# Projections with their loads ahead of the key arrays, and attention sums with the attention term broadcast as rows

## The chip, the cores and the metric

The kernel runs on one core of a Trainium2 chip. The metric is device time of one execution in microseconds (us): the median of three timed runs. One further execution was taken by the hardware profiler; all rows of the trace come from it.

## The reference

Two graph layers over 12500 nodes of 256 numbers and 200000 edges, sorted by `dst`:

```python
# layer 0: attention of each node `dst` over its edges
enh = x + 0.1 * query_emb
Q, K, V = enh @ Wq + bq, enh @ Wk + bk, enh @ Wv + bv           # (N, 4 heads, 64)
scores = sum_d Q[dst] * (K[src] + 0.2 * rel_w[edge_type]) / 8   # one per edge and head
w = softmax of scores over the edges of one dst
msgs = segment_sum(w * V[src], dst)                             # V where a node has no edge
y = layernorm(msgs @ Wo + bo + x) * gamma + beta
x = layernorm(x + y)
# layer 1: sums over the edges of one src
x_i, x_j = leaky(x @ W1 + b1), leaky(x @ W2 + b2)
a1, a2 = x_i @ wa1 + ba1, x_j @ wa2 + ba2
att = sigmoid(a1[src] + a2[dst])                                # one per edge
x = layernorm(2 * x + segment_sum(att * x_j[dst], src))
```

## The kernel before

Nodes lie in 98 blocks of 128; a table in SBUF, `node_tab`, holds 260 columns for each block. Edges are sorted by the node that they are summed into and cut into tiles of 128. Merged with the block borders they give 1664 steps: one tile against one block, four steps (U) to a group, 416 groups (G). The stages follow one another, each a block of the program with a barrier behind it:

1. `project` (L200 to L392): Q into `node_tab`, K and V to DRAM as `kv_rows`. At the same time VectorE starts to sort 200000 keys (node pair, for the second layer), 1024 columns to an operation.
2. `build_steps` for layer 0: which block each step works on (`places`), the local number of each edge's node (`local`), the other end of each edge (`other`).
3. `edge_scores`: GpSimd gathers K and V of each step by indirect DMA (L645), TensorE picks Q rows with a one-hot, VectorE multiplies and reduces and, between groups, goes on with the key sort (L717, L719).
4. `softmax_numerators`, then `aggregate`: V rows weighed by ScalarE and GpSimd, summed by TensorE with a one-hot (L1027) and added to `node_tab` by VectorE (L1006).
5. `build_steps` for layer 1, `update_nodes`: Wo, two layer norms, W1 and W2, a1 in `a1_tab` (one column to a block), rows x_j with a2 as column 256 to DRAM as `xj_rows`.
6. `attend`: the sums of layer 1, then `finish`: the last layer norm.

In `project`, SyncE first issues the loads of the key arrays (after GpSimd has padded them), `keys[n][0:97]` at L243 and the rest at L244, then weights and biases (L247, L248), the query column (L250) and the blocks of x (L254), two in flight. GpSimd splits the biases into three bf16 parts. For each block TensorE turns x (L339), ScalarE adds 0.1 query on the way from PSUM (L310), TensorE multiplies by Wk, Wv (L352, 512 columns) and Wq (L352, 256 columns) and adds the bias by a matmul of ones with the three parts (L353, one for K and V, one for q). ScalarE evacuates q scaled by 1/8 (L317) and K, V (L319), GpSimd stores them (L295). There is one PSUM tile for turned x and one for q, two for K, V.

In `attend`, the groups pass through the engines with these hand-overs. GpSimd gathers four times 128 rows of `xj_rows` (L1340) into a ring of RING = 6 groups; before group g it waits for the sum of group g - 6. VectorE makes the one-hot of the local number against `iota` (L1371, two groups ahead), TensorE turns it (L1407), ScalarE copies the turned one (L1360), TensorE multiplies it with the block's column of `a1_tab` (L1427): a1 of each edge. VectorE adds a2 (L1377), ScalarE takes the sigmoid (L1348) and scales the one-hot with it (L1353), TensorE sums 128 rows of x_j with it (L1415, each fp32 product is two matmul records), VectorE adds the result to `node_tab` (L1386), whose place is loaded to registers from `places1`. TensorE's order is turn(g + 1), lookup(g), sum(g - 1); VectorE's is one-hot(g + 2), a2 of g, add(g - 2).

## Time and profile before

| | us |
|---|---|
| median of 3 timed runs | 7487.49 |
| lowest, highest | 7469.43, 7493.04 |
| the profiled execution | 7541.05 |
| its span, first to last instruction | 7539.4 |
| busy: TensorE 71%, VectorE 60%, GpSimd 55%, ScalarE 41% of the span | 5366.9, 4547.7, 4117.2, 3080.2 |

Engines in the rows: PE is TensorE (PEld its weight loads), DVE VectorE, ACT ScalarE, POOL GpSimd, SP SyncE; SPq is SyncE's own queue, which issues DMAs. L352 is line 352 of the kernel before. Busy time is that of the engine, so an issue of an indirect DMA on POOL counts, one on SPq does not. Times of the trace are counted from the first instruction.

### The profile page before, as it was taken

The page shows a single profiled execution, that of the slowest core. Times are in us where ns is not written, and L with a number is a line of the kernel's source. Part 1 is how long each engine was busy: PE and PEld are TensorE (multiplying, and loading weights), DVE is VectorE, ACT ScalarE, POOL GpSimd, SP SyncE. Part 2 cuts the span into 40 slices and gives each one's busy share as a digit, 9 for nine tenths or more (in the row PEclk, how much of TensorE's full clock was granted, in tenths as well). Part 3 has the DMA queues.
Part 4 walks back from the last instruction along what each step waited for, and adds up shares of the span by engine and source line. Part 5 has one row for each costly group of instructions (what it writes and reads, how often), then busy time and mean ns, then how long its engine had stood idle before and what let it go on. Part 6 is the DMA issues. An engine that isn't in the chain of part 4 may idle for free. (4 is left out here: it accounts for less than half of the span.)

```text
span 7539.4 us, 82733 instructions
## 1 busy us (share of the span) xinstructions
PE 5366.9 (71%) x21563; PEld 4019.8 (53%) x21563; DVE 4547.7 (60%) x8352; ACT 3080.2 (41%) x8260; POOL 4117.2 (55%) x4183
## 2 busy tenths in 40 slices
PE   5966666666667556637777768877777777777874
PEld 2445555555555444425555544446666666666663
DVE  6216666767677555578888878964444444444446
ACT  2323333333333333328777754433333333333333
POOL 1126666666667555513333325556666666666663
PEclk9976776767666676669999999987777777777776
DMA  2348888888898888816666643323333333333333
GB/s 74 106 146 281 276 292 285 276 287 289 291 299 290 287 280 275 274 36 199 199 199 199 199 142 88 88 78 92 91 91 91 91 91 91 91 91 91 91 92 112
DMA packets 857534, 1308.71 MB, mean 174 GB/s; under 512 B 87145, under 2 KB 690535, under 8 KB 856787
## 3 DMA queue, kind: packets, MB, share of 16 engines
q0 software_dynamic: 221008, 683.55, 29.1%
q1 hardware_dynamic: 629091, 613.77, 26.1%
q10 hardware_dynamic: 7010, 6.38, 0.2%
q8 instruction: 187, 3.06, 0.2%
q14 instruction: 238, 1.95, 0.1%
HBM read 1031.10 MB, written 272.26 MB: 173 GB/s over the span
## 5 line engine op out<-in xcount | busy, mean ns | idle before, releaser
L645 POOL DMA_INDIRECT s_rows<-kv_rows,other x1664 | 1737.3, 1044 | 949.3 <-issue 496.1
L1340 POOL DMA_INDIRECT t_rows<-xj_rows,other x1664 | 1626.0, 977 | 837.5 <-issue 444.6
L1415 PE MATMUL ps_xsum<-t_rows,t_hot_att 128*128 128x256 f32 x3328 | 1235.7, 536 | 417.5 <-DVE node_tab L1386 388.7
L754 PE MATMUL ps_rel<-rel,hot 64*128 64x64 f32 x3328 | 613.0, 341 | 862.6 <-DVE s_rows L737 628.5
L756 PE MATMUL ps_q<-node_tab,hot 128*128 x3328 | 1191.6, 518 | 36.1 <-issue 35.6
L1415 PEld LDWEIGHTS ps_xsum<-t_rows,t_hot_att 128*128 128x128 f32 x3328 | 863.8, 272 | 594.6 <-issue 356.1
L754 PEld LDWEIGHTS ps_rel<-rel,hot 64*128 64x128 f32 x3328 | 552.3, 249 | 1057.2 <-issue 969.3
L734 DVE TENSOR_TENSOR s_rows<-s_rows,ps_rel 128x1024 f32<-128x1024 f32 x416 | 506.4, 1217 | 931.8 <-remote 706.7
L661 ACT ACTIVATE hot<-apart,ones 128x1024 f32<-128x1024 bf16 x416 | 477.8, 1148 | 1373.3 <-remote 767.7
L1027 PE MATMUL ps_sum<-a_terms,a_hot 128*128 128x260 f32 x3328 | 830.1, 392 | 282.7 <-DVE node_tab L1006 193.3
L756 PEld LDWEIGHTS ps_q<-node_tab,hot 128*128 128x128 f32 x3328 | 817.3, 258 | 221.0 <-issue 42.6
L987 ACT ACTIVATE a_terms<-a_terms,score 128x64 f32<-128x64 f32 x3328 | 839.8, 334 | 218.8 <-DMA a_terms<-v_edges 218.1
L1386 DVE TENSOR_TENSOR node_tab<-node_tab,ps_xsum 128x256 f32 x1664 | 699.9, 421 | 363.1 <-issue 181.1
L1027 PEld LDWEIGHTS ps_sum<-a_terms,a_hot 128*128 128x128 f32 x3328 | 599.3, 190 | 513.3 <-issue 430.2
L1006 DVE TENSOR_TENSOR node_tab<-node_tab,ps_sum 128x260 f32 x1664 | 703.5, 423 | 183.0 <-DVE node_tab L1006 5.4
L972 POOL TENSOR_TENSOR a_terms<-a_terms,score 128x512 f32<-128x512 f32 x416 | 438.2, 1053 | 661.6 <-DMA a_terms<-v_edges 661.6
L1377 DVE TENSOR_TENSOR t_logit<-ps_a,t_rows 128x4 f32<-128x4 f32 x416 | 67.4, 162 | 1084.0 <-DMA x_in<-in_x 1036.4
L1360 ACT COPY t_node_hot<-ps_hot 128x512 f32<-128x512 f32 x416 | 243.8, 586 | 915.9 <-remote 831.9
L656 ACT ACTIVATE apart<-apart,minus_p 128x1024 bf16<-128x1024 bf16 x416 | 473.4, 1138 | 326.6 <-DMA apart<-what_rows 239.4
L1353 ACT ACTIVATE t_hot_att<-t_hot,t_att 128x128 f32<-128x128 f32 x1664 | 531.6, 390 | 13.6
L737 DVE TENSOR_TENSOR s_rows<-s_rows,ps_q 128x1024 f32<-128x1024 f32 x416 | 507.8, 1221 | 14.2
L739 DVE TENSOR_REDUCE score<-s_rows 128x16 f32<-128x1024 f32 x416 | 507.4, 1220 | 14.2
(208 smaller groups left out, 5835.0 us busy)
## 6 DMA issues: line engine op xcount, KB each, us to landing
v_edges<-s_rows SPq DMA_DIRECT2D x416, 512.0 KB
a_terms<-v_edges SPq DMA_DIRECT2D x416, 512.0 KB, 3.7
apart<-what_rows SPq DMA_DIRECT2D x416, 256.0 KB
s_rows<-kv_rows,other POOLq DMA_INDIRECT x1664
t_rows<-xj_rows,other POOLq DMA_INDIRECT x1664
kv_rows<-kv_out POOLq DMA_DIRECT2D x97, 256.0 KB, 2.3
xj_rows<-n_hx SPq DMA_DIRECT2D x97, 130.0 KB, 2.1
x_in<-in_x SPq DMA_DIRECT2D x97, 128.0 KB, 2.0
```

The costliest lines, as they stand in the source:

```text
L645: pool.indirect_dma_start(out=rows[g % KV_RING][:, k, :], out_offset=None, in_=t["kv_rows"], in_offset=bass.IndirectOffsetOnAxis(ap=t["oth ...
L737: dve.tensor_tensor(key, key, ps_q[g % 2][:, :, :], ALU.mult).then_inc(picked_used, 1)
L739: dve.tensor_reduce(t["score"][:, g * U * H:(g + 1) * U * H].rearrange("p (k h) -> p k h", h=H), by_head, AX.X, ALU.add)\
L754: nc.tensor.matmul(ps_rel[g % 2][:, k, :], hot[g % 2][0:R, 1, k, :], rel_02[:, :], start=True, stop=True)
L756: last = nc.tensor.matmul(ps_q[g % 2][:, k, :], hot[g % 2][:, 0, k, :], t["node_tab"][:, bass.ds(blocks[k] * AW, D)], start=True, stop=True)
L987: last = nc.scalar.activation(head, head, ACT.Copy, scale=t["score"][:, at:at + 1])
L1006: dve.tensor_tensor(acc, acc, ps_sum[g % 2][:, k, 0:AW], ALU.add).then_inc(added, 1)
L1027: last = nc.tensor.matmul(ps_sum[g % 2][:, k, 0:AW], hot[g % 4][:, k, :], terms[g % DEEP][:, k, :], start=True, stop=True)
L1340: pool.indirect_dma_start(out=rows[g % RING][:, k, :], out_offset=None, in_=t["xj_rows"], in_offset=bass.IndirectOffsetOnAxis(ap=t["other1 ...
L1353: last = nc.scalar.activation(hot_att[g % 2][:, k, :], hot[g % 4][:, k, :], ACT.Copy, scale=att[g % 2][:, k:k + 1])
L1386: dve.tensor_tensor(acc, acc, ps_sum[g % 2][:, k, :], ALU.add).then_inc(added, 1)
L1415: last = nc.tensor.matmul(ps_sum[g % 2][:, k, :], hot_att[g % 2][:, k, :], rows[g % RING][:, k, 0:D], start=True, stop=True)
```

## The change

In `project`: SyncE issues block 0 of x, the query column and the weights first, then three more blocks of x, the three biases broadcast to 128 partitions, and then the keys, each array as 96 rows, one row and the rest; it also issues the stores of K and V, from four buffers instead of two. x has four buffers, all three kinds of PSUM tile have two. The bias matmuls and the bf16 parts are gone: VectorE evacuates K and V with a tensor_tensor that adds the bias, and q with a scalar_tensor_tensor that scales and adds. The key sort is a generator, of which VectorE runs one operation after each K/V evacuation and, in two blocks of three, one more after q, from block 6 on.

In `build_steps` for layer 1, one operation makes `block_hot`: for each step a column with a 1 at its block. In `attend`, a1 is turned to rows (98 x 128), multiplied by `block_hot` to one row of 128 for each step, and stored to DRAM as `a1_rows`. For each group SyncE broadcasts four of these rows to all partitions, eight groups in flight. ScalarE takes sigmoid(a1 row + a2 of the gathered edge) over 128x128; VectorE multiplies it with the one-hot in one scalar_tensor_tensor, in place; TensorE sums. All hand-overs are by step, VectorE's adds lag three groups and alternate with the weighing, PSUM has four tiles, the ring of gathered rows RING = 14 groups. The lookup of a1 by TensorE, its copy and the logits are gone. Tiles of layer 0 are given back sooner, and `update_nodes` has a scratch tile of its own.

```diff
-RING = 6
+RING = 14
+ATT_RING = 8
@@ project, SyncE
+            load(0)
+                sp.dma_start(q_col[:, :], query.rearrange("(c p) -> p c", p=P)).then_inc(weights_in, 16)
+            for n, w in ((1, wk), (2, wv), (0, wq)):
+                sp.dma_start(w_qkv[:, :, n * D:(n + 1) * D], w.rearrange("(c p) n -> p c n", p=P)).then_inc(weights_in, 16)
+            for b in range(1, 4):
+                load(b)
+            for n, a in enumerate((bq, bk, bv)):
+                sp.dma_start(b_wide[:, n * D:(n + 1) * D], a.partition_broadcast(P)).then_inc(biases_in, 16)
             sp.wait_ge(pads_set, 1)
             for n, a in enumerate((t["src"], t["dst"])):
-                sp.dma_start(keys[n][0:full_p, :], a[0:full_p * F].rearrange("(p f) -> p f", f=F)).then_inc(keys_in, 16)
+                sp.dma_start(keys[n][0:even_p, :], a[0:even_p * F].rearrange("(p f) -> p f", f=F)).then_inc(keys_in, 16)
+                sp.dma_start(keys[n][even_p:full_p, :], a[even_p * F:full_p * F].rearrange("(p f) -> p f", f=F)).then_inc(keys_in, 16)
...
+            for b in range(NB):
+                if b + 4 < NB:
+                    sp.wait_ge(xt_ready, b + 1)
+                    load(b + 4)
+                r = rows_of(b)
+                sp.wait_ge(kv_ready, b + 1)
+                sp.dma_start(t["kv_rows"][b * P:b * P + r, :], kv_out[b % 4][0:r, :]).then_inc(kv_stored[b % 4], 16)
@@ project, TensorE
-                        nc.tensor.matmul(o, enh[u][:, c, :], w_qkv[:, c, lo:hi], start=(c == 0), stop=False)
-                    last = nc.tensor.matmul(o, t["ones_h"][0:3, :], b_parts[:, lo:hi], start=False, stop=True)
+                    last = nc.tensor.matmul(ps_kv[b % 2][:, :], enh[b % 2][:, c, :], w_qkv[:, c, D:3 * D], start=(c == 0), stop=(c == 1))
...
+                    last = nc.tensor.matmul(ps_q[b % 2][:, :], enh[b % 2][:, c, :], w_qkv[:, c, 0:D], start=(c == 0), stop=(c == 1))
@@ project, VectorE
+            for b in range(NB):
+                dve.wait_ge(kv_done, b + 1)
+                if b >= 4:
+                    dve.wait_ge(kv_stored[b % 4], 16 * (b // 4))
+                dve.tensor_tensor(kv_out[b % 4][:, :], ps_kv[b % 2][:, :], b_wide[:, D:3 * D], ALU.add).then_inc(kv_ready, 1)
+                if b >= 6:
+                    next(sorting, None)
+                dve.wait_ge(q_done, b + 1)
+                dve.scalar_tensor_tensor(tab[:, b * AW:b * AW + D], ps_q[b % 2][:, :], float(DH) ** -0.5, b_wide[:, 0:D],
+                                         ALU.mult, ALU.add).then_inc(q_kept, 1)
+                if b >= 6 and b % 3:
+                    next(sorting, None)
+            for _ in sorting:
+                pass
@@ build_steps
+            if layer:
+                step(dve.tensor_scalar(t["block_hot"][:, :], row, partition[:, 0:1], None, ALU.is_equal))
@@ attend, SyncE
+            for n, (lo, hi) in enumerate(halves):
+                sp.wait_ge(a1_copied, n + 1)
+                sp.dma_start(t["a1_rows"][lo * P:hi * P, :].rearrange("(c p) e -> p c e", p=P), a1_steps[:, lo:hi, :]).then_inc(a1_stored, 16)
+            sp.wait_ge(a1_stored, 2 * 16)
+            for g in range(G):
+                if g >= ATT_RING:
+                    sp.wait_ge(summed, (g - ATT_RING + 1) * U)
+                sp.dma_start(att[g % ATT_RING][:, :, :].rearrange("p k e -> p (k e)"),
+                             t["a1_rows"][g * U:(g + 1) * U, :].rearrange("k e -> (k e)").partition_broadcast(P)).then_inc(a1_in[g % ATT_RING], 16)
@@ attend, GpSimd
-                    pool.wait_ge(summed, g - RING + 1)
+                    pool.wait_ge(summed, (g - RING + 1) * U)
@@ attend, ScalarE
+                act.wait_ge(a1_in[g % ATT_RING], 16 * (g // ATT_RING + 1))
+                act.wait_ge(rows_in[g % RING], 16 * U * (g // RING + 1))
                 for k in range(U):
+                    last = nc.scalar.activation(att[g % ATT_RING][:, k, :], att[g % ATT_RING][:, k, :], ACT.Sigmoid,
+                                                bias=rows[g % RING][:, k, D:D + 1])
+                last.then_inc(att_ready, 1)
@@ attend, VectorE
+            def weigh(g, k):
+                if k == 0:
+                    dve.wait_ge(att_ready, g + 1)
+                w = att[g % ATT_RING][:, k, :]
+                dve.scalar_tensor_tensor(w, t["iota"][:, :], t["local1"][:, g * U + k:g * U + k + 1], w, ALU.is_equal, ALU.mult)\
+                    .then_inc(hot_att_ready, 1)
+
+            def add(g, k, block):
+                acc = tab[:, bass.ds(block * AW, D)]
+                dve.wait_ge(summed, g * U + k - k % 2 + 2)
+                if g * U + k:
+                    dve.wait_ge(added, g * U + k)
+                dve.tensor_tensor(acc, acc, ps_sum[g % 4][:, k, :], ALU.add).then_inc(added, 1)
+
+            for g in range(G + 3):
+                if g >= 3:
+                    blocks = blocks_of(nc, dve, t["places1"], g - 3)
                 for k in range(U):
+                    if g < G:
+                        weigh(g, k)
+                    if g >= 3:
+                        add(g - 3, k, blocks[k])
@@ attend, TensorE
+            nc.tensor.transpose(ps_a1, t["a1_tab"][:, :], t["ident"][:, :]).then_inc(a1_turned, 1)
+            pe.wait_ge(a1_staged, 1)
+            for n, (lo, hi) in enumerate(halves):
+                for c in range(lo, hi):
+                    last = nc.tensor.matmul(ps_steps[n][:, c - lo, :], t["block_hot"][0:NB, c * P:(c + 1) * P], a1_stage[:, :], start=True, stop=True)
+                last.then_inc(a1_spread, 1)
+            pe.wait_ge(a1_copied, 2)
+            for g in range(G):
                 for k in range(U):
+                    pe.wait_ge(hot_att_ready, g * U + k + 1)
+                    if g >= 4:
+                        pe.wait_ge(added, (g - 4) * U + k - k % 2 + 2)
+                    nc.tensor.matmul(ps_sum[g % 4][:, k, :], att[g % ATT_RING][:, k, :], rows[g % RING][:, k, 0:D], start=True, stop=True)\
+                        .then_inc(summed, 1)
```

## Rows read from the trace of the kernel before

**Rows 1.** Busy time by stretch: stretch, us, engines' busy us, clock, DMA share, GB/s.
```profile
77.00:445.00 368.00, 363.50 (x1176) 168.72 (x1176) 161.72 (x142) 136.32 (x392) 53.07 (x98) 1.00 0.30 104
...
3367.00:4480.00 1113.00, 830.11 (x3328) 599.34 (x3328) 928.84 (x2080) 876.61 (x3743) 438.17 (x416) 1.00 0.63 197
...
4994.00:7459.00 2465.00, 1900.60 (x8320) 1593.41 (x8320) 1017.67 (x2496) 841.38 (x2497) 1625.95 (x1664) 0.74 0.34 91
```

**Rows 2.** Waits of the first 77 us: total us, times, longest.
```profile
ACT q L304 <- DMA q_col<-in_L_gnn_query_emb: 69.0, 1, 69.0
DVE keys L367 <- DMA keys<-in_dst: 68.5, 1, 68.5
```

**Rows 3.** Timeline of the start: start us, us, engine, line, work.
```profile
13.98 28.33 SPq L244 DMA_DIRECT2D keys<-in_dst  x1
...
60.33 2.41 SPq L250 DMA_DIRECT2D q_col<-in_L_gnn_query_emb  x1
...
79.14 3.62 PE L352 MATMUL ps_kv<-w_qkv,enh 128*128 128x512 f32 x4
```

**Rows 4.** Timeline of TensorE over one block of the projections.
```profile
92.70 1.88 PE L352 MATMUL ps_kv<-w_qkv,enh 128*128 128x512 f32 x4
...
94.51 0.39 PE L353 MATMUL ps_kv<-b_parts,ones_h 3*128 3x512 bf16 x1
...
94.83 1.13 PE L352 MATMUL ps_q<-w_qkv,enh 128*128 128x256 f32 x4
...
95.89 0.28 PE L353 MATMUL ps_q<-b_parts,ones_h 3*128 3x256 bf16 x1
...
96.10 0.44 PE L339 MATMUL ps_xt<-ident,x_in 128*128 128x128 f32 x2
...
96.38 1.88 PE L352 MATMUL ps_kv<-w_qkv,enh 128*128 128x512 f32 x4
```

**Rows 5.** Timeline of the next stage's start, three loads of 768 KB.
```profile
454.64 0.38 SPq L452 DMA_DIRECT2D score<-in_dst  x1
...
466.09 0.17 DVE L506 TENSOR_SCALAR last_block<-score 128x13 int32<-128x13 int32 x1 [224.78 <-DMA score<-in_edge_type]
```

**Rows 6.** Timeline of VectorE and GpSimd: attention sums, then edge scores.
```profile
6002.22 0.95 POOL L1340 DMA_INDIRECT t_rows<-xj_rows,other  x1 [0.31 <-issue]
6002.33 0.68 DVE L1371 TENSOR_TENSOR t_hot<-iota,local 128x512 f32<-128x512 f32 x1
...
6008.24 0.68 DVE L1371 TENSOR_TENSOR t_hot<-iota,local 128x512 f32<-128x512 f32 x1
...
6008.48 1.27 POOL L1340 DMA_INDIRECT t_rows<-xj_rows,other  x1 [0.30 <-issue]
...
1011.00 1.22 DVE L717 TENSOR_TENSOR keys<-keys 128x1024 f32<-128x1024 f32 x1
...
1011.07 1.96 POOL L645 DMA_INDIRECT s_rows<-kv_rows,other  x1 [0.30 <-issue]
```

**Rows 7.** Timeline of GpSimd in the attention sums, a gather that waited.
```profile
6035.14 0.95 POOL L1340 DMA_INDIRECT t_rows<-xj_rows,other  x1 [1.83 <-PE ps_xsum L1415]
```

**Rows 8.** Groups of instructions by line: shapes, count, busy us, mean ns, idle before.
```profile
L1386 DVE TENSOR_TENSOR node_tab<-node_tab,ps_xsum 128x256 f32 x1664 | 699.9, 421 | 363.1 <-issue 181.1 <-DVE node_tab L1386 3.4 <-remote 1.2
...
L1353 ACT ACTIVATE t_hot_att<-t_hot,t_att 128x128 f32<-128x128 f32 x1664 | 531.6, 390 | 13.6
...
L1231 DVE TENSOR_TENSOR n_hx<-ps_h,n_hx 128x512 f32<-128x512 f32 x98 | 66.4, 678 | 7.1 <-ACT n_hx L1145 7.0
...
L1298 DVE SCALAR_TENSOR_TENSOR score<-n_v,n_alone,score 128x256 f32<-128x256 f32 x98 | 43.9, 448 | 0.1
```

**Rows 9.** Two lines of the sums: ns min/median/max, first and last start us.
```profile
L1371 DVE TENSOR_TENSOR t_hot<-iota,local x416: 681/684/694, 4993.8 to 7443.8; 128x512 f32<-128x512 f32 x139
...
L1340 POOL DMA_INDIRECT t_rows<-xj_rows,other x1664: 940/947/1554, 4994.5 to 7439.0; - x185
```

**Rows 10.** Timeline, the last adds of the attention sums.
```profile
7456.67 2.11 DVE L1386 TENSOR_TENSOR node_tab<-node_tab,ps_xsum 128x256 f32 x4 [0.21 <-DVE node_tab L1386]
```

More of the change, by code:

```diff
@@ L204, in sb, with pb @@
             return ctx.enter_context(nc.sbuf_tensor(name, shape, dt))
+        def pb(name, shape):
+            return [ctx.enter_context(nc.psum_tensor(f"{name}{u}", shape, fp32)) for u in range(2)]
         def sem(name):
@@ L227, in project @@
[L227 to L233 removed]
+        b_wide = sb("b_wide", [P, 3 * D])
@@ L356, in _, with transpose @@
-            transpose(0, 0)
-            block_pairs(pe, body)
+            def transpose(b):
+                pe.wait_ge(x_loaded[b % 4], 16 * (b // 4 + 1))
+                if b >= 2:
+                    pe.wait_ge(enh_ready, b - 1)
+                for c in range(2):
+                    last = nc.tensor.transpose(ps_xt[b % 2][:, c, :], x_in[b % 4][:, c * P:(c + 1) * P], ident[:, :])
+                last.then_inc(xt_ready, 1)
+            pe.wait_ge(consts_set, 1)
+            transpose(0)
@@ L393, in _, with sort @@
-            assert now == MERGES[0][1]
+            def sort():
+                step = Serial(dve, key_step)
+                dve.wait_ge(keys_in, 6 * 16)
+                dve.wait_ge(consts_set, 2)
+                dve.tensor_scalar(keys[0][:, :], keys[0][:, :], NODE_BITS, KEY_BIAS, ALU.logical_shift_left, ALU.bitwise_or).then_inc(key_step, 1)
+                yield
+                dve.wait_ge(key_step, 1)
+                dve.tensor_tensor(keys[0][:, :], keys[0][:, :], keys[1][:, :], ALU.bitwise_or).then_inc(key_step, 1)
+                yield
+                step.n = 2
+                for m in range(7):
+                    step(dve.tensor_scalar(pbit[:, m:m + 1], pid[:, :], m, 1, ALU.logical_shift_right, ALU.bitwise_and))
+                step(dve.tensor_scalar(sign[:, 0:7], pbit[:, 0:7], -2.0, 1.0, ALU.mult, ALU.add))
+                step(dve.memset(sign[:, 7:8], 1.0))
+                step(dve.tensor_tensor(two_signs[:, 0:7], sign[:, 0:7], sign[:, 1:8], ALU.mult))
+                yield
+                done, now = step.n, 0
+                for k in range(1, FREE + 1):
+                    z = pair[now]
+                    if k == 1:
+                        v = z.rearrange("p (n s w) -> p n s w", s=2, w=2)[:, :, 1, :]
+                    elif k < FREE:
+                        v = z.rearrange("p (n s w) -> p n s w", s=4, w=1 << (k - 1))[:, :, 1:3, :]
+                    else:
+                        v = z[:, F // 2:F]
+                    dve.wait_ge(key_step, done)
+                    dve.tensor_scalar(v, v, -1.0, None, ALU.mult).then_inc(key_step, 1)
+                    done += 1
+                    yield
+                    if k == FREE:
+                        dve.wait_ge(key_step, done)
+                        dve.tensor_scalar(z, z, sign[:, 0:1], None, ALU.mult).then_inc(key_step, 1)
+                        done += 1
+                        yield
+                    for j in range(k - 1, -1, -1):
+                        a, b = (v.rearrange("p (n two d) -> p n two d", two=2, d=1 << j) for v in (pair[now], pair[1 - now]))
+                        dve.wait_ge(key_step, done)
+                        dve.tensor_tensor(b[:, :, 0, :], a[:, :, 0, :], a[:, :, 1, :], ALU.min)
+                        yield
+                        dve.tensor_tensor(b[:, :, 1, :], a[:, :, 0, :], a[:, :, 1, :], ALU.max).then_inc(key_step, 1)
+                        done += 1
+                        now = 1 - now
+                        yield
+                assert now == MERGES[0][1]
+                dve.wait_ge(key_step, done)
@@ new lines, in _ @@
+            sorting = sort()
+            dve.wait_ge(biases_in, 3 * 16)
+            dve.wait_ge(bias_ready, 1)
+            for b in range(NB):
+                dve.wait_ge(kv_done, b + 1)
[9 more added lines that the diff above has]
+                    next(sorting, None)
@@ L1328, in attend @@
[L1328 to L1332 removed]
+        att = [sb(f"t_att{u}", [P, U, P]) for u in range(ATT_RING)]
@@ new lines, in attend @@
+        a1_stage, a1_steps = sb("t_a1_stage", [NB, P]), sb("t_a1_steps", [P, C, P])
+        ps_sum = [ctx.enter_context(nc.psum_tensor(f"ps_xsum{u}", [P, U, D], fp32)) for u in range(4)]
+        ps_a1 = ps_sum[3][0:NB, 0, 0:P]
+        ps_steps = [ps_sum[u][:, :, :].rearrange("p k (two e) -> p (k two) e", e=P) for u in range(2)]
+        halves = ((0, 8), (8, C))
+        rows_in, a1_in = [sem(f"t_rows_in{u}") for u in range(RING)], [sem(f"t_a1_in{u}") for u in range(ATT_RING)]
+        a1_turned, a1_staged, a1_spread, a1_copied, a1_stored = (sem(f"t_a1_{n}") for n in ("turned", "staged", "spread", "copied", "stored"))
@@ L1388, in _ @@
-            encode(0)
-            encode(1)
-            for g in range(G):
-                if g + 2 < G:
-                    encode(g + 2)
-                add_logits(g)
-                if g >= LAG:
-                    add(g - LAG)
-            for g in range(G - LAG, G):
-                add(g)
+            def weigh(g, k):
[4 more added lines that the diff above has]
+                    .then_inc(hot_att_ready, 1)
```

253 lines of the change are left out of this document (60 added, 193 removed).

## The prediction, made before the changed kernel was run

> **What bounds the kernel now.** I read the stage table first. Cut by stage, the span shows two stretches that the change rewrites: the first stage, up to 445 us, and the attention sums from 4994 to 7459 us, 2465 us or 33% of the span [rows 1]. The other stages (edge scores, softmax, first aggregation, node update, finish) keep their code.
>
> The waits of the start come next: ScalarE sat 69.0 us for the query column, VectorE 68.5 us for the keys [rows 2]. The timeline says why: SyncE puts the two key arrays into its queue first, one issue alone takes 28.33 us, the query column goes out at 60.33 and the first K/V projection starts at 79.14 [rows 3]. After that TensorE is busy 363.5 of 368 us [rows 1]: the projections are bound by TensorE, one block of 128 nodes every 3.68 us (92.70 to 96.38) [rows 4]. VectorE is not the bound there: its key sort ended 224.78 us before 466.09, at 241.3 [rows 5].
>
> In the attention sums no engine is full: TensorE 1901, GpSimd 1626, VectorE 1018, ScalarE 841 of 2465 us [rows 1]. A group of four steps takes 2465/416 = 5.93 us. GpSimd issues gathers 1.25 us apart (0.95 and 0.30 between) as long as it need not wait [rows 6], and about once in eight gathers waits 1.8 us for a sum to free a ring place [rows 7]. So the pace comes from the loop TensorE (turn the one-hot, look up a1, sum) to ScalarE to VectorE and back. TensorE at its mean granted clock of 0.74 [rows 1] is close to full there: this loop, and not the gathers, ends last.
>
> **First stage: the loads.** In the new order block 0 of x, the query column and the three weights go out before anything else, and the keys last. Nothing waits for a 776 KB transfer any more. The query column takes 2.41 us to issue [rows 3]; a large load 0.38 us, and three of 768 KB landed 11.4 us after the first of their issues [rows 5], so 0.9 MB of x and weights need some 5 us. From a first issue near 1 us that gives 8 to 10, and I take 12 since each piece is small; the first K/V matmul then at 13 instead of 79.14 (1 us for the scaled column and the enhanced block 0). Bounds: 9 (the 8 us and the same 1) and 25 (x and weights share the queues with the keys). Gain 66 us, 54 to 70.
>
> **First stage: the blocks.** Both bias matmuls go: from 94.51 to 94.83 and from 95.89 to 96.10, 0.32 + 0.21 us of each period [rows 4]. 3.68 - 0.53 = 3.15; I take 3.2. VectorE takes over what ScalarE evacuated: the K/V add reads 512 columns of PSUM as L1231 does, 0.68 us, and q some 0.43 (L1298 has 0.45 for 256 columns, L1386 0.42) [rows 8]. With the sort (241.3 - 68.5 = 173 us over its 92 blocks, 1.88) that is 0.68 + 0.43 + 1.88 = 2.99 us a block, under 3.2 with PSUM two deep. The cover is thin, 0.2 us; if it is gone, VectorE sets 3.5 (0.68 + 0.43 + two sort operations of 1.2) and the stage gains 32 us less. 147 sort operations have 153 places, so none is left over. The keys must be there at block 6, at 13 + 6 x 3.2 = 32 us: in the next stage three loads of 768 KB, each split as the keys now are, were all there 11.4 us after the first issue (454.64 to 466.09) [rows 5], so two take some 8 us and land near 25. SyncE now also issues the stores of K/V; a store has two blocks of slack and GpSimd's issuing of them was hidden before. Blocks: 98 x 0.48 = 47 us. Together 66 + 47 = 113 us; from 54 + 18 = 72 to 70 + 52 = 122.
>
> A rule of the Trainium skill lies beside the 28.33 us: DMA: Bandwidth & Descriptors, on why a DMA increments its semaphore by 16, says that a copy is split over the largest number of engines up to 16 that divides its slowest dimension, thus 97 rows on one engine and 96 on sixteen. The keys' split into 96 + 1 rows would by it be quick; were it wrong, they would land near 70 us and hold VectorE, and through it TensorE, at block 6 for about 38 us, a third of the stage's gain. The three loads of [rows 5] are of the 128-row kind and bear the rule out.
>
> **Between.** `block_hot` is one tensor_scalar over 128x1664 on VectorE's path: 1 us, bounded by 0.3 and 2. The scratch tile, the other places of tiles and the longer list of semaphores to clear: 0 to 1 us each; 0.
>
> **Attention sums: what goes.** The encode (0.68 us), the 4 transposes and 8 lookup matmuls of a group, the copy and the logit go; TensorE keeps the 8 passes of the sum. In their place SyncE broadcasts 256 KB a group, ScalarE does four sigmoids of 128x128 (L1353 has 0.39 us each, 1.56 a group), VectorE four scalar_tensor_tensor of 128x128. L1298 takes 0.448 us for 256 columns; at 1.05 ns a column (1.22 us for 1024 columns, 0.684 for 512) [rows 6, 9] half of them is 0.31 us [rows 8].
>
> What sets the pace then? VectorE: 4 x (0.31 + 0.42) + 0.34 for the register loads + some 0.1 for each of 8 waits = 4.1 us, bounded by 3.3 (no gaps) and 5.3 (0.3 us of gap on every weigh, 0.15 on every add). TensorE: the first aggregation has the same 8 passes, the same adds and an encode besides, and took 1113/416 = 2.68 us a group at clock 1.00 [rows 1]; at half clock twice that share of it that is matmul, 830/416 x 2 = 4.0 us. ScalarE 1.6. DMA: 0.34 busy now at 91 GB/s [rows 1]; the rows add 256 KB per 5 us, 51 GB/s, so 0.6 at most. GpSimd: 4 x 1.252 = 5.01 us. All others lie below it, so GpSimd becomes the bound, and with 14 groups in the ring (70 us of gathers) it never waits for a sum: the 15 us that the a1 rows need to be spread, stored and read back (two copies of about 1 us, 26 passes, a store and a load of 3 to 4 us each) are hidden behind gathers that start at once. Without that cover they would cost their 15 us once.
>
> **Attention sums: the gather against VectorE.** A gather reads its indices from SBUF. Where an encode, which has two SBUF inputs, had started 0.24 us before a gather, the gather took 1.27 instead of 0.95 us; where the encode started 0.11 us after it, it took 0.95 [rows 6]. The same in the edge scores: an exchange of the key sort at 1011.00, the gather at 1011.07 took 1.96, until 0.8 us after the exchange had ended at 1012.22 [rows 6]. So a gather is held only if such an operation runs about 0.1 us after its start, and by what is left of it. The new weigh has two SBUF inputs as well, four of 0.31 us a group. At random phase 0.31/1.25 = 25% of gathers lose half of 0.31: 0.04 us each, 64 us in all. Bounds: nothing (the phase is locked, the weighs fall between the reads), and 0.31 on every gather, 516 us. I take 64, since the phase is locked to the landing of the rows and at most one or two of four read moments meet a weigh.
>
> SBUF — State Buffer of the Trainium skill, on its two separate sides, states more: the shared pair is an exclusive lock that whoever starts first holds for the whole instruction. Read so, a gather would also hold a weigh, up to 0.95 us. Here no encode was ever longer than 0.694 us, with one beginning 0.11 us into a gather [rows 6, 9]; the trace does not bear that half out for gathers. By the rule VectorE would need 0.36 us more a weigh (0.76 of the time inside a gather, 0.47 on average): 5.5 us a group, 200 us more than the sum below; that is part of the rival on VectorE's pace.
>
> **The sum.** First gather to last: 1663 x 1.252 + 64 = 2146 us instead of 7439.0 - 4994.5 = 2444.5 [rows 9], gain 298 (0 to 362 without the worst phase). Behind the last gather now come 20 us (the last adds end at 7458.8) [rows 10]; then landing 3, sigmoids 1.5, four weighs 3.5, the adds of three more groups 8.5: 17, gain 3. In all 113 + 298 + 3 - 1 = 413 us. The profiled execution took 7541 us (span 7539.4), so its successor takes 7128. The median of the three timed runs is 7487.5, 53.6 us below the profiled one; the same difference off it gives **7075 us**.
>
> **Rivals.** *VectorE or TensorE sets the pace of the sums* (semaphore round trips on each of 16 steps' hand-overs, or the half of the lock that I set aside): 5.3 to 5.6 us a group instead of 5.16, 60 to 190 us more; 7200. For it: three engines now pass each single step on; against it the 2.68 us of the first aggregation. *The first stage gains only its start*: VectorE, with the sort between the adds, holds TensorE at 3.5 to 3.7 us a block, or the keys come late: 7075 + 40 = 7115. *The other side*: each gather is met by a weigh. Phase is locked, so a bad phase would stay for all 416 groups. From 0.29 us a gather on (478 us over 1664) everything is lost; at 0.31 on each the sums take 2600 + 17 us, and the kernel 7075 + 452 = 7527, slower. Against it: a weigh of 0.31 us would have to begin just before every read, while weighs come some 0.9 us apart and gathers 1.25.
>
> **How the numbers follow.** Forecast 0.74 (own range 7010 to 7150), VectorE's or TensorE's pace 0.13, first stage short 0.09, the gathers all held 0.02, something else that costs over 400 us 0.02. What a measurement can tell from no change is 0.3%, 22 us. Faster 0.96, same 0.01, slower 0.03. The range for 8 in 10 is 7000 to 7210: its low end has no held gather and a stage at 3.1 us a block, its high end reaches into the paced rival.
>
> **What would show it.** Right: the first K/V matmul before 20 us and blocks 3.2 us apart; in the sums GpSimd busy about 0.76 of the stage, its gaps 0.30 us almost throughout, the group at 5.0 to 5.2 us, no wait for a sum; gathers with a second length up to 1.26 us. Wrong: gathers waiting for sums again; weighs longer than 0.35 us or starting late behind a gather; K/V adds that TensorE waits for; a stage of sums above 2300 us.

## The result, and the profile of the changed kernel

| | before | after |
|---|---|---|
| median, same chip | 7487.0 (4 runs) | 7281.5 (4 runs) |
| ratio, 95% interval | | 0.972 (0.971 to 0.974) |
| span of the profiled execution | 7539.4 | 7282.5 |
| first gather of the edge scores begins | 508.3 | 342.3 |
| first gather of the edge scores to the end of the last | 2686 | 2655 |
| first gather of the attention sums to the end of the last | 2445.5 | 2370.0 |

The gain is 205.5 us, where 413 were forecast. The profile of before lies 54 us above its median, so the traces differ by 257: 166 before the first gather of the edge scores, 31 in the edge scores, whose code is the same, 67 in the sums up to their last matmul, less 7 lost in the other stages.

The first stage did more than forecast. Its timeline in the changed kernel (start us, us, engine, line, work; the answer to [rows 3, 4]):

```profile
7.15 0.20 ACT L292 ACTIVATE q<-q_col 128x2 f32<-128x2 f32 x1 [5.13 <-DMA w_qkv<-in_L_gnn_Wq]
...
8.06 3.78 PE L325 MATMUL ps_node_kv<-w_qkv,enh 128*128 128x512 f32 x4
...
22.49 1.88 PE L325 MATMUL ps_node_kv<-w_qkv,enh 128*128 128x512 f32 x4
24.21 1.03 PE L330 MATMUL ps_node_q<-w_qkv,enh 128*128 128x256 f32 x4
25.07 0.38 PE L312 MATMUL ps_xt<-ident,x_in 128*128 128x128 f32 x2
25.29 1.02 PE L325 MATMUL ps_node_kv<-w_qkv,enh 128*128 128x512 f32 x2
```

The first K/V matmul starts at 8.06 instead of 79.14, and a block takes 2.80 us (22.49 to 25.29) instead of 3.68. By stretch, as in [rows 1] (stretch and its length, then busy us of TensorE, its weight loads, VectorE, ScalarE and GpSimd, each with its instructions; granted clock, DMA share, GB/s):

```profile
8.00:285.00 277.00, 276.36 (x977) 166.26 (x976) 255.38 (x351) 61.07 (x196) 0.00 (x0) 1.00 0.45 143
...
4810.00:7160.00 2350.00, 1195.02 (x3226) 729.47 (x3226) 1060.46 (x3214) 504.21 (x1632) 1580.48 (x1648) 0.66 0.49 140
```

TensorE is full in the first stage, VectorE nearly. In the sums nothing is: GpSimd 67%, TensorE 51%, VectorE 45%. A group takes 5.70 us, not the 5.16 of the forecast. The lines of the sums (the answer to [rows 8, 9]), and what GpSimd waited for between 4810 and 7160 (us in total, times, longest):

```profile
L1359 POOL DMA_INDIRECT t_rows<-xj_rows,other x1664 | 1595.9, 959 | 792.0 <-issue 470.7
...
L1392 DVE TENSOR_TENSOR node_tab<-node_tab,ps_xsum 128x256 f32 x1664 | 699.6, 420 | 1227.9 <-remote 848.4
...
L1384 DVE SCALAR_TENSOR_TENSOR t_att<-iota,local,t_att 128x128 f32<-128x128 f32 x1664 | 578.2, 348 | 77.8 <-issue 46.2
```

```profile
POOL t_rows L1359 <- issue: 466.4, 1526, 0.8
POOL t_rows L1359 <- remote: 248.1, 83, 9.2
POOL t_rows L1359 <- PE ps_xsum L1418: 51.7, 39, 4.1
```

No gather is held by VectorE (959 ns against 977), no weigh by a gather (348 ns). But GpSimd waits for sums again, with 14 places in its ring, and VectorE's adds wait 848 us for something that the profile calls "remote". The timeline shows such a wait:

```profile
5989.60 1.33 PE L1418 MATMUL ps_xsum<-t_rows,t_att 128*128 128x256 f32 x4 [1.04 <-issue]
5989.83 0.35 DVE L1384 SCALAR_TENSOR_TENSOR t_att<-iota,local,t_att 128x128 f32<-128x128 f32 x1
5990.21 0.96 POOL L1359 DMA_INDIRECT t_rows<-xj_rows,other  x1 [0.30 <-issue]
...
5995.27 0.95 POOL L1359 DMA_INDIRECT t_rows<-xj_rows,other  x1 [0.30 <-issue]
5996.48 0.32 SPq L1350 DMA_DIRECT2D t_att<-a_rows  x1
5996.53 0.96 POOL L1359 DMA_INDIRECT t_rows<-xj_rows,other  x1 [0.30 <-issue]
5996.59 0.42 DVE L1392 TENSOR_TENSOR node_tab<-node_tab,ps_xsum 128x256 f32 x1 [6.41 <-remote]
```

From 5990.9 to 5996.5 every engine but GpSimd stands still, and SyncE and VectorE go on together. VectorE was waiting for the sum of three groups back, whose matmul had ended at 5983.4, as had 11 later sums by 5991. So I compared the semaphore updates in the trace with the ends of the instructions that make them. An update is what an engine adds to a semaphore, its report to the others. In the stages without gathers an update comes 0.01 to 0.02 us after its instruction, on every engine. In the stages where GpSimd gathers, TensorE's come late, and TensorE's alone: in the changed sums 2.7 us behind the latest matmul at the median and 8.3 at the 95th percentile, VectorE's and ScalarE's 0.01 us (as far as their updates are recorded). The kernel before has it too, at the median 3.8 us behind the latest lookup, 2.6 behind the latest transpose, 1.5 behind the latest sum. There GpSimd paused after each eighth gather (205 times) and the updates came 1.5 us after that gather's end. What it waited for between 5010 and 7430:

```profile
POOL t_rows L1340 <- issue: 439.7, 1442, 0.4
POOL t_rows L1340 <- remote: 239.0, 129, 4.1
POOL t_rows L1340 <- PE ps_xsum L1415: 134.2, 75, 2.1
```

I had read these waits [rows 7] as a busy loop of engines.

### The profile page after: what moved, and what is told of

It reads as the page before. It is cut to its first block and busy times, and to the rows that moved or that the text cites. A ratio compares the mean times of both kernels' runs of the same rounds, so it can differ in the third digit from the quotient of the medians.

```text
span 7282.5 us, 70497 instructions
## 1 busy us (share of the span) xinstructions
PE 4567.1 (63%) x16402; PEld 3136.6 (43%) x16402; DVE 4715.6 (65%) x9381; ACT 2684.0 (37%) x7236; POOL 4037.0 (55%) x4077
## 5 line engine op out<-in xcount | busy, mean ns | idle before, releaser
L1359 POOL DMA_INDIRECT t_rows<-xj_rows,other x1664 | 1595.9, 959 | 792.0 <-issue 470.7
L1418 PE MATMUL ps_xsum<-t_rows,t_att 128*128 128x256 f32 x3328 | 1228.0, 516 | 1161.2 <-DVE t_att L1384 624.3
L1418 PEld LDWEIGHTS ps_xsum<-t_rows,t_att 128*128 128x128 f32 x3328 | 746.1, 248 | 1642.9 <-DVE t_att L1384 794.1
L1374 ACT ACTIVATE t_att<-t_att,t_rows 128x128 f32<-128x128 f32 x1664 | 514.0, 388 | 1856.7 <-DMA t_att<-a_rows 1615.4
L765 PE MATMUL ps_q<-node_tab,hot 128*128 x3328 | 1162.4, 507 | 39.6 <-issue 38.8
L763 PE MATMUL ps_rel<-rel,hot 64*128 64x64 f32 x3328 | 592.8, 333 | 861.8 <-DVE s_rows L746 648.4
L763 PEld LDWEIGHTS ps_rel<-rel,hot 64*128 64x128 f32 x3328 | 533.3, 241 | 1053.3 <-issue 947.1
L765 PEld LDWEIGHTS ps_q<-node_tab,hot 128*128 128x128 f32 x3328 | 797.7, 252 | 218.7 <-issue 48.3
L1384 DVE SCALAR_TENSOR_TENSOR t_att<-iota,local,t_att 128x128 f32<-128x128 f32 x1664 | 578.2, 348 | 77.8 <-issue 46.2
L1005 DVE TENSOR_TENSOR a_hot<-iota,keys 128x512 f32<-128x512 f32 x416 | 286.9, 690 | 0.0
```

Of the source, the lines that this page charges most:

```text
L763: nc.tensor.matmul(ps_rel[g % 2][:, k, :], hot[g % 2][0:R, 1, k, :], rel_02[:, :], start=True, stop=True)
L765: last = nc.tensor.matmul(ps_q[g % 2][:, k, :], hot[g % 2][:, 0, k, :], t["node_tab"][:, bass.ds(blocks[k] * AW, D)], start=True, stop=True)
L1359: pool.indirect_dma_start(out=rows[g % RING][:, k, :], out_offset=None, in_=t["xj_rows"], in_offset=bass.IndirectOffsetOnAxis(ap=t["other1 ...
L1374: last = nc.scalar.activation(att[g % ATT_RING][:, k, :], att[g % ATT_RING][:, k, :], ACT.Sigmoid, bias=rows[g % RING][:, k, D:D + 1])
L1384: dve.scalar_tensor_tensor(w, t["iota"][:, :], t["local1"][:, g * U + k:g * U + k + 1], w, ALU.is_equal, ALU.mult)\
L1418: nc.tensor.matmul(ps_sum[g % 4][:, k, :], att[g % ATT_RING][:, k, :], rows[g % RING][:, k, 0:D], start=True, stop=True)\
```

## The experiments

The sets ran on five chips, numbered 10, 3, 11, 14 and 4; each kernel is compared with the kernel before on its own chip. The changed kernel as it stands ran on chips 3 and 4; on 11 and 14 its figures are those of the first comparison, whose kernel before took nearly the same time (7487.0 beside 7492.4 and 7475.5). The expectations in us for set 1 were made for a chip where the kernel before takes 7487.

**Set 1, chip 10: each half alone, fewer reports, no gathers.** `e1` has the new first stage with the old sums, `e2` the reverse.

> The new first stage with the old attention sums (ring of 6). The traces of before and after put 195 us before the first gather of the attention sums. If that is so and independent of the sums: 7487 - 195 = 7292 us (7280 to 7310), blocks again 2.80 us apart. If by the forecast's sizes: 7374. If part of the gain came by way of the other edit, nearer 7400.

> The old first stage with the new attention sums. If the sums gave 75 us whatever stands before them: 7487 - 75 = 7412 us (7400 to 7430), the sums again some 2370 us from first to last gather. By the forecast (gathers set the pace): 7186.

`e3`:

```diff
-                    nc.tensor.matmul(ps_sum[g % 4][:, k, :], ...).then_inc(summed, 1)
+                    last = nc.tensor.matmul(ps_sum[g % 4][:, k, :], ...)
+                last.then_inc(summed, 1)
```

> The kernel after, but TensorE reports its sums once a group (on the last matmul) instead of once a step; VectorE, SyncE and GpSimd wait by group. Theory A (each TensorE semaphore update is held up while gathers are issued, and the updates queue up, so their number sets the pace): 416 updates instead of 1664, the sums fall toward the gathers' own 2100 us, the kernel to 7000 to 7100. Rival B (the hold-up is a delay of some us that does not depend on the number of updates): 7270 to 7300, as after. Rival C (TensorE's half clock after pauses is the cause): 7270 to 7320, or slower, since the adds of a group now start later.

`e4`:

```diff
-                    pool.indirect_dma_start(out=rows[g % RING][:, k, :], ..., in_=t["xj_rows"], ...)
+                    sp.dma_start(rows[g % RING][:, k, :], t["xj_rows"][lo:lo + P, :])
```

> The kernel after with the gathers of the attention sums left out: SyncE loads as many rows (128 rows of 1040 bytes a step, contiguous, other rows than the right ones), GpSimd stands still. It tells whether the gathers or something among the engines keeps TensorE's reports back. Theory A: TensorE's updates come within 0.1 us of its matmuls, a group takes 2.7 to 3.5 us, the kernel 6100 to 6400. Rival C (clock) or a fault of the hand-overs themselves: the stalls stay, a group takes some 5.7 us, 7250 to 7300. Rival D (amount of DMA traffic, the broadcasts among it, delays the updates): lags of some us stay, since the traffic per group is the same.

Measured: the kernel before takes 6677.1 us on this chip. e1 6543.2, ratio 0.980 (0.978 to 0.982); e2 6685.5, 1.001 (1.000 to 1.002); e3 6552.5, 0.981 (0.980 to 0.983); e4 5534, with 2.57 us a group in the sums. No update of TensorE is later than 0.02 us in any stage of any of them, so the set could not part A from B; it showed something else. Old sums (e1) and new sums (e3), stretches of nearly the same length:

```profile
4355.00:6440.00 2085.00, 1676.81 (x8260) 1456.12 (x8259) 1007.82 (x2473) 825.09 (x2479) 1581.64 (x1653) 0.82 0.40 106
```

```profile
4355.00:6445.00 2090.00, 1334.90 (x3304) 792.15 (x3304) 1062.65 (x3292) 528.22 (x1655) 1586.70 (x1653) 0.73 0.59 158
```

Both make 1653 gathers, 1.26 us apart without a pause: 2100 and 2105 us. That is the pace that I had forecast for the new sums, but the old ones have it as well, so the new ones gain nothing. The new first stage gives only 134 us here, though the first gather of the edge scores comes 165 us earlier in e3 than in e2: in e1 and e3 gathers lie 1.261 us apart, in e2 1.251, which makes 29 us over both stages of gathers. Why the pitch differs between programs no run shows. The clock is down to half for part of the time here too (a mean of 0.73 in e3), with no stall: theory C is out.

**Set 2, chip 3: the changed kernel, and the same again.**

> The changed kernel unaltered, beside the kernel before. The first four experiments ran where the kernel before takes 6677 us, not 7487, and where TensorE's semaphore updates come 0.02 us after its matmuls in every stage. If this run is of that kind too: gathers at their own pace in both kernels (1664 x 1.26 = 2100 us), so only the first stage counts, 6677 - 126 = 6551 us, a ratio of 0.981. If it is of the kind of the first comparison (late updates): 7280, ratio 0.972.

> One report of TensorE a group, once more, beside the unaltered kernel. Where TensorE's updates are not late: as the unaltered kernel within 5 us. Where they are late: theory A (updates queue up, their number counts) 7000 to 7150; rival B (a delay that does not depend on their number) within 20 us of the unaltered kernel.

> New first stage, old attention sums, once more, beside the others. Where TensorE's updates are not late: 6543, the sums of both kernels paced by the gathers. Where they are late: 7487 - 195 = 7292, and the distance to the unaltered changed kernel is what the new sums give by themselves (some 75 us less the 15 of spreading a1).

`e8` is e4 with the plain loads on GpSimd (`pool.dma_start`).

> The gathers of the attention sums left out: GpSimd loads as many rows by plain copies of 128 contiguous rows (other rows than the right ones). Where TensorE's updates are late in the other kernels: still late here if any transfer issued by GpSimd does it, 0.02 us if it is the indirect form alone. Where they are not late: the group at the pace of GpSimd's issue of a plain copy, about 0.55 + 0.3 us each, 3.4 us a group, or VectorE's 3.3: some 700 us below the unaltered kernel.

Measured: before 7533.2; e5 7334.4, 0.973 (0.971 to 0.976); e6 7335.0, 0.973 (0.972 to 0.975); e7 7372.3, 0.979 (0.978 to 0.981); e8 5999.7 (one execution). This chip has the late updates. A quarter of the reports changes nothing: theory A has fallen. On one chip the new first stage gives 161 us, not the 195 that e7 was expected to show, and the new sums 38. And in e8 the same TensorE reports are 0.02 us late at most, though the edge scores of the same execution have them 8.7 us late (95th percentile, behind TensorE's latest instruction):

```profile
4820.00:5870.00 1050.00, 1024.53 (x3206) 479.67 (x3206) 1029.26 (x3196) 518.79 (x1624) 865.65 (x1636) 0.99 0.96 311
```

GpSimd issues 1636 plain copies, DMA is 96% busy, and a group takes 2.56 us. So it takes the indirect form; traffic and copies from GpSimd do not do it. The row also shows that the other engines need less than half the gathers' time for a group, at a granted clock of 0.99.

One kernel on two chips shows how far the matter reaches. Of e3 and e6, the same program, the trace holds 8872 semaphore updates in 500 us of the sums on chip 10 and 1091 on chip 3 (4900 to 5400 us), landings of DMAs among them; from 8 to 285 us, where nothing gathers, 3799 and 3797.

**Set 3, chip 11: pauses, ring, more TensorE work, half the gathers.** `e9`, and `e10` with `RING = 6`:

```diff
-                if g >= RING:
-                    pool.wait_ge(summed, (g - RING + 1) * U)
+                if g >= 8 and g % 4 == 0:
+                    pool.wait_ge(summed, (g - 4) * U)
```

> The kernel after with GpSimd's wait changed: no wait for a ring place 14 groups back, but before every fourth group a wait for all sums up to four groups back. Where TensorE's updates are late: theory E (they come through when GpSimd stops issuing gathers; in the kernel before they came 1.5 us after each eighth gather) gives a pause of about 2 us every 16 gathers, 5.04 + 0.5 = 5.5 us a group instead of 5.76, 60 to 110 us less than the kernel after (7220 where that is 7334). Rival B (a fixed delay after each update, whatever GpSimd does): as the kernel after or up to 150 us slower, since GpSimd now waits for the newest sums. Where they are not late: GpSimd hardly ever waits, as the kernel after.

> The kernel after with 6 instead of 14 groups of gathered rows. Where TensorE's updates are late: by theory E a full ring makes GpSimd pause sooner and oftener, which lets the updates through, so no more than 1% slower, perhaps faster; by the ring's own logic (more places, fewer waits for sums) 50 to 150 us slower. Where they are not late: the sums are some 5 us behind the gathers, 6 groups are enough, within 5 us of the kernel after.

`e11` and `e12`:

```diff
+                    for _ in range(2):
+                        nc.tensor.matmul(ps_sum[g % 4][:, k, 0:1], att[...][:, k, :], rows[...][:, k, 0:1], ...)
```

```diff
+                    if k % 2:
+                        pool.dma_start(rows[g % RING][:, k, :], t["xj_rows"][lo:lo + P, :]).then_inc(...)
+                        continue
```

> The kernel after with two idle matmuls of one column ahead of each sum (their result is overwritten), without updates: twice as many TensorE instructions more, no more semaphore traffic. Where updates are late: theory F (what holds them up is every TensorE instruction's completion, not only the reported ones) 200 us or more above the kernel after; if only gathers and pauses matter, within 40 us. Where they are not late: TensorE has room for 4 x 0.4 us a group, within 10 us.

> Every second gather of the sums left out: its rows come by a plain GpSimd copy of 128 contiguous rows (other rows than the right ones). GpSimd needs 2 x 1.26 + 2 x 0.65 = 3.8 us a group. Where updates are late and every gather holds them: lags of some us stay, 4.3 to 4.8 us a group. If it takes an unbroken run of gathers to hold them: lags under 1 us, 3.8 us a group.

Measured: before 7492.4; e9 7265.3, 0.970 (0.968 to 0.972); e10 7263.8, 0.969 (0.966 to 0.971); e11 7773.5, 1.038 (1.036 to 1.040); e12 6461 (one execution). In e9 the reports are less late (4.6 us at the 95th percentile instead of 8.3), and still the gathers take 2375 us, in e10 2369, in the changed kernel of the first comparison 2370. So pauses of the kernel's own choice do not shorten the stage (theory E had 7220 us), nor do more places in the ring. e11 and e12:

```profile
4800.00:7580.00 2780.00, 2734.29 (x9610) 2445.51 (x9610) 1090.05 (x3209) 518.09 (x1619) 1591.81 (x1640) 0.50 0.43 117
```

```profile
4820.00:6340.00 1520.00, 1115.93 (x3261) 625.85 (x3260) 1048.98 (x3248) 519.73 (x1628) 1274.59 (x1620) 0.87 0.76 214
```

In e11 TensorE is full at the half clock (2734 of 2780 us) and sets 6.77 us a group; its reports are on time. The 508 us over e9 are TensorE's own work; my estimate that it had room for it was wrong (why the clock stays at half here and at 0.99 in e8, where TensorE is as full, no run shows). Theory F, that each instruction's completion is held up, has fallen: there are more than twice as many, and 95% of the reports come within 0.02 us. In e12 GpSimd sets 3.73 us a group with two gathers in it; reports on time too. Late reports, then, need neither many TensorE instructions nor gathers as such. They come where gathers would run faster than they did in the kernels so far, 5.70 us for four, 1.425 us each. Whether that is a rate at which something serves them, these runs do not show.

**Set 4, chip 14: room between gathers, no broadcast.**

```diff
                         .then_inc(rows_in[g % RING], 16)
+                    nc.gpsimd.memset(pace[:, g * U + k:g * U + k + 1], 0)
```

> The kernel after with a memset of one byte a partition on GpSimd behind every gather of the sums (some 0.10 us each, plus 0.05 of gap). Where TensorE's updates are late: theory G (an unbroken run of gathers 1.26 us apart holds them; a little air lets them through) gives 4 x (1.26 + 0.13) = 5.55 us a group without late updates, 60 to 90 us less than the kernel after. Theory H (they need real pauses, some 0.66 us a group whatever their place, as the kernel after, the one with 6 places and the one with a wait each fourth group all came to 5.70 us a group) leaves 5.7 us a group, within 20 us of the kernel after. If the memsets themselves add to what is held up: slower by up to 200 us. Where updates are not late: 0.5 us a group more, 200 us slower than the kernel after.

> The same, and also behind three of four gathers of the edge scores. There a group takes 6.4 us where updates are late and 5.3 where they are not. Theory G: 5.33 + 0.4 = 5.75 us a group in the edge scores, some 270 us less, with the sums 340 us below the kernel after. Theory H: edge scores as before, within 30 us of the kernel above.

> The kernel after with the broadcasts of a1 left out from the ninth group on (the att tiles keep what was last in them, so the terms are wrong): ScalarE waits for the sum eight groups back in SyncE's place. DMA carries 256 KB less a group. If the amount of transfer or SyncE's increments add to the hold-up: 5.0 to 5.4 us a group where updates are late, 100 us or more less. If gathers alone make it: 5.7 us a group, within 20 us.

Measured: before 7475.5; e13 7276.6, 0.974 (0.971 to 0.977); e14 7283.3, 0.974 (0.971 to 0.978); e15 7259 (one execution). e13 and e14 do not test what they were made for: the memset ran in the 0.30 us that lie between two gathers anyway, and their pitch stayed 1.26 us, in the edge scores too (2649 us in e14, 2644 in e13). e15 moves 94 GB/s instead of 140 at the same 5.70 us a group, so the broadcasts have no part. What the kernels have in common is the sum of GpSimd's pauses beyond its pitch of 1.26 us: 265 us in the changed kernel (90 pauses), 263 with 6 places (92), 263 in e9 (73), 269 in e13 (103), 266 in e15 (84). Chips 3 and 4 have other sums, but again nearly the same one for both of their kernels: 293 us in e5 and 298 in e6, 277 in e17 and in e18 (see set 5). Only the old order of the sums waits longer (360 us before, 353 in e7). So in the new order, wherever the waits are put, some 265 to 300 us have to be waited.

The packets of the gathers say what it is not. In e10, on chip 11, the last packet of a gather ends 1.5 us after its issue at the median and 3.0 at the 95th percentile, and ScalarE starts on a group 0.43 us after the group's last packet; in e3, on chip 10, it is 1.9, 2.8 and 0.43 us. In the changed kernel's unbroken runs the lag of the packets does not grow (1.0 us after the ninth gather of a run as after the eighteenth). So the gathers are not served late, and their own reports are on time; TensorE's alone are not.

**Set 5, chip 4: a slower GpSimd, and the ring.** `e16` is e13 with `RING = 6` and four memsets.

> Ring of 6 and four memsets of one byte a partition behind every gather. One memset alone (0.12 us) vanished in the 0.30 us between two gathers, whose pitch stayed 1.26; four should make it 1.5 us, 6.0 us a group. Theory H in its last form (where updates are late, something serves the gathers at 1.425 us each, 5.70 a group, and lets reports wait while it is behind; GpSimd pauses sum to 265 us whatever the ring): GpSimd now is slower than that, so no pauses, no late updates (0.02 us), and the sums take 416 x 6.0 = 2500 us, 130 us above the kernel after. If instead every gather holds reports up by itself: still late updates, pauses on top, 2600 us or more. Where updates are not late: 2500 us as well.

> The kernel after with 6 groups of gathered rows, beside the kernel after. By theory H the pace is the same; only the queue behind the last gather differs (last sum 10.3 us behind it instead of 24.8 in the first comparison): 10 to 20 us less than the kernel after. Where updates are not late: equal within 5 us.

> The kernel after, beside the two above. 7280 to 7340 where updates are late (ratio 0.973), 6551 where they are not (ratio 0.981).

Measured: before 7519.6; e16 7332.4, 0.975 (0.973 to 0.977); e17 7285.8, 0.969 (0.968 to 0.971); e18 7307.7, 0.972 (0.970 to 0.974). e16 missed its pitch again: the four memsets overlap, the gathers are 1.31 us apart. The stretch between 5502 and 5507 on GpSimd:

```profile
5502.22 0.96 POOL L1360 DMA_INDIRECT t_rows<-xj_rows,other  x1
5503.17 0.24 POOL L1364 MEMSET t_pace<- 128x1 uint8 x4
5504.91 0.95 POOL L1360 DMA_INDIRECT t_rows<-xj_rows,other  x1 [1.49 <-issue]
5505.86 0.20 POOL L1364 MEMSET t_pace<- 128x1 uint8 x4
5506.21 0.96 POOL L1360 DMA_INDIRECT t_rows<-xj_rows,other  x1
```

Here GpSimd stops by itself before the second gather of a group, where the program has no wait, and of its 188 pauses of over 0.5 us 100 stand before such gathers; they make 122 us of 252. TensorE's reports, as far as they are recorded, are nearly on time (0.01 us late at the median, 0.94 at the 95th percentile). In the kernels without memsets the pauses stand before a group's first gather, where the program waits for a sum. The pauses counted as above still sum to 247 us and a group takes 5.84 us, where e17, without memsets, has 277 and 5.73. That speaks against a fixed rate as well: at e17's 1.43 us a gather, a pitch of 1.31 would leave some 210 us to wait. Which engine is stopped changes; that something is stopped for nearly as long does not. The condition of the test (a GpSimd slower than 5.70 us a group) was not reached, only e11 and e12 stand on that side.

The ring of 14 costs a little: e17 is 22 us below e18. Its gathers take as long (2383.5 and 2382.7 us), but the last matmul ends 9.8 us after the last gather instead of 29.2, since fewer groups are queued behind it. With a ratio of 0.969 this kernel (e10 and e17) is the fastest found where updates are late, with e9 (0.970) inside its interval.

## Why the prediction was wrong, step by step

**First stage, loads: right.** First K/V matmul at 8.06, forecast 13 and just under the lower bound of 9; the weights were the last to land, and the keys were there in time for block 6, split as they are.

**First stage, blocks: right mechanism, a term too small.** 3.2 forecast, 2.80 measured, 85 us instead of 47. The bias matmuls took with them 0.53 us of their own, as worked out, and 0.35 of their neighbours: K/V to the next start 1.81 to 1.72, q 1.06 to 0.86, transposes 0.28 to 0.22 ([rows 4] and the timeline above). VectorE's cover held: 255 of 277 us busy, 14.9 us of waits for K/V products. Start and blocks make 156 of the 166 us. The other 10 lie between the last projection and the first load of the next stage (441.5 to 454.6 before, 285.5 to 288.7 after); the forecast had nothing for them. GpSimd issued the stores of K and V before, SyncE does now; whether that is the reason no run separates.

**Sums, the other engines: below the gathers, as forecast, but the sizes were too large.** VectorE 4.1 us a group with a lower bound of 3.3, TensorE 2.68 to 4.0 were forecast; e8 shows them all together at 2.56. A weigh takes 0.35 us (0.31 forecast), but it and the add behind it overlap: a pair starts every 0.64 us in e8.

**Sums, gathers held by weighs (64 us): wrong, nothing.** The mean gather is 959 ns, the longest 1096. Nor did gathers hold weighs: 348 ns beside gathers, 347 beside plain copies in e8. The half of the lock in SBUF — State Buffer of the Trainium skill (its two separate sides) that the forecast set aside is not borne out for indirect gathers here. (Its price was wrong too: 0.36 us more a weigh gives some 150 us by the forecast's own terms, not 200.)

**Sums, the pace: the step that failed.** "GpSimd: 4 x 1.252 = 5.01 us. All others lie below it, so GpSimd becomes the bound". The 1.252 us is the pitch between two waits, and I took it for a pace that can be kept. On four of the five chips of the experiments, and on the one of the first comparison, it can't. Nor is it true that with 14 groups in the ring GpSimd never waits for a sum: it waited for reports of TensorE that came late, 90 pauses and 265 us in all, and the gathers came to 1.425 us each over the stage (1.42 to 1.46 in all kernels with the new order and four gathers). With 1.425 the term is 1664 x 1.425 = 2371 instead of 2146. On chip 10 the forecast's term holds (2105, without the 64), but there it holds for the kernel before as well, and the sums gain nothing (e2).

**Sums, the kernel before: misread.** I took its 5.93 us a group for a loop of busy engines. Late reports paced it as well, at 5.88 from first to last gather, where the new order has 5.70 and, on chips 3 and 4, 5.73 to 5.76. The difference to the changed kernel, 75 us, has two parts. Shorter pauses make 45. The other 30 are gathers that no encode holds any more: 182 gathers of the kernel before took over 1.05 us, nearly all begun 0.25 to 0.32 us after an encode, and the mean fell from 977 to 959 ns. The forecast had seen such a gather [rows 6] and not counted what taking the encode out would give. I had taken the clock of 0.74 to put TensorE near its limit, and did not ask why matmuls that had ended were waited for. On chip 10 the old sums, with the same loop, run at 5.05: the loop never was the bound. The rival on VectorE's or TensorE's pace named 5.3 to 5.6 us a group and semaphore round trips; the size is near, but a quarter of the reports (e6) changes nothing.

**Tail:** 3 us less were forecast; it is 9 us longer (24.8 us from the last gather to the last matmul instead of 16.3), for the ring: with 6 places it is 10 us (e10, e17).

## What to carry to other kernels

The pitch of an operation between two waits is not its pace over a stage: divide the stage by the count (before: 2445/1664 = 1.47 us, not 1.25) and explain the difference before calling it free. Where an engine waits for another, look whether the other had long been done; if it had, the wait belongs to neither, and moving work between the two gives nothing. Where rings, waits and traffic are changed and the pauses keep their sum, the limit lies outside the kernel's own order of work; what sets it is then still to be found.

## What the runs showed of the hardware that I had not expected

- With GpSimd issuing indirect gathers of 128 rows, TensorE's semaphore updates come late (edge scores: 8.2 to 8.9 us behind its latest instruction at the 95th percentile), on chips 3, 11, 14 and 4; on chip 10 never. The same kernel before takes 6677 us there and 7476 to 7533 on the others; edge scores (gathers of 2 KB rows) and sums make up the difference: 467 and 345 us between e1 and the profile of before, of some 810.
- In the changed kernel's sums 472 of 3602 register and semaphore instructions of VectorE take 0.68 to 0.74 us, most of the others under 0.1. There are none such in e3, but also none in the kernel before and in e7, whose reports are late too. Many late reports are spaced by 0.68 to 0.74 us (173 of 1400) or come in bursts 0.04 us apart (615).
- Over a stage a gather takes 1.42 to 1.46 us with rows of 1 KB (new sums) and 1.59 to 1.61 with rows of 2 KB (edge scores) where reports are late; on chip 10 1.26 and 1.33. What limits the edge scores is not separated: on chip 10 the DMA engines are full there (100% at 345 GB/s in e3), elsewhere GpSimd waits for VectorE (416 us in the changed kernel).

What it is that holds TensorE's reports while gathers are issued, what sets the sum of the pauses, and why chip 10 is free of it, stays open. Every run here was recorded with its span and clock, so none tells whether the recording of events takes part. Two signs would fit it: most update records of the late stages are missing, and in the changed kernel instructions of VectorE that need nothing last 0.71 us. One speaks against the number of records as the cause: on chip 3 the sums of e8 left 36 update records in each us, with no report late, and those of e5 2.6; on chip 10, with none lost, the sums of e3 left 18. The Trainium skill, NOTIFIC — Programmer's Manual, When the ring fills, says that a queue of records can lose new ones or stall the engine that makes them; no run here shows that it does. Not tried: gathers of fewer rows or shorter rows, which would part the number of descriptors from the bytes.
